# Edge stage of a graph attention kernel: gathers wait on VectorE's messages of the pair six back

## What is computed

```python
Q, K, V = (x @ W for W in (Wq, Wk, Wv))            # 6250 x 512, 8 heads of 64
score = einsum('ehd,ehd->eh', K[src], Q[dst]) / 8
score = exp(clip(score, -5, 5))[..., None]
msg = V[src] * score
wV, Z = segment_sum(msg, dst), segment_sum(score, dst)
h = x + wV / (Z + 1e-6)
y = (h - mean(h, 0)) * rsqrt(var(h, 0) + 1e-5) * gamma + beta
out = layernorm(x + y, axis=-1)
```

## Time and profile before

| | us |
|---|---|
| median of three runs | 1907.17 |
| profiled execution | 1908.01 |
| its span, first to last instruction | 1906.1 |
| edge stage, first gather to last sums | 452 to 1760 |

### The profile page before, as it was taken

How to read it: one execution, slowest core, us unless ns; L and a number is a source line. 1 busy time by engine, 2 the same in 40 slices (tenths; PEclk the granted TensorE clock), 3 DMA queues, 4 the chain that set the end, 5 groups by cost and what they waited for, 6 DMA issues and landing times.

```text
span 1906.1 us, 41424 instructions
## 1 busy us (share of the span) xinstructions
PE 1861.6 (98%) x7904; PEld 1362.2 (71%) x8014; DVE 1697.0 (89%) x2454; ACT 1367.5 (72%) x4602; POOL 1291.3 (68%) x1473
## 2 busy tenths in 40 slices
PE   7999999998999999999999999999999999999897
PEld 4555555554888888878888888888888888887333
DVE  6677755644999999999999999999999999999888
ACT  0002000002999999999999999999999999998857
POOL 0205666103777888788888888888888888885677
PEclk9999999999999999999999999999999999999999
DMA  5547788546999999999999999999999999999307
GB/s 183 162 151 250 288 319 274 186 161 231 357 358 356 362 367 358 346 351 368 368 356 353 352 366 369 354 355 355 366 361 358 360 355 365 370 358 370 122 33 287
DMA packets 184521, 589.09 MB, mean 309 GB/s; under 512 B 28480, under 2 KB 30240, under 8 KB 184480
## 3 DMA queue, kind: packets, MB, share of 16 engines
q0 software_dynamic: 135904, 465.14, 65.8%
q1 hardware_dynamic: 45120, 121.69, 17.8%
q10 hardware_dynamic: 3456, 1.78, 0.3%
HBM read 535.27 MB, written 78.91 MB: 322 GB/s over the span
## 4 chain that ended last, share of the span: by engine, by line
PE 74%; DVE 16%; issue 4%; DMA 4%; ACT 1%; POOL 1%; SPq 0%; DVEq 0%; ACTq 0%; POOLq 0%
PE acc L939 29%; PE places L342 22%; PE q_ps L923 17%; DVE kv L795 6%; DVE raw L806 5%; DMA kv<-kv_d,idx 2%; PE mm_ps L949 2%; PE banks L1151 1%; DVE stats L1288 1%; DVE agg L1281 1%; PE mm_ps L951 1%; PE places L402 1%; DMA q_tile<-xb_d 1%; POOL kv L751 1%; PE banks L1142 1%
## 5 line engine op out<-in xcount | busy, mean ns | idle before, releaser
L751 POOL DMA_INDIRECT kv<-kv_d,idx x880 | 887.0, 1008 | 339.2 <-issue 204.8
L846 ACT ACTIVATE kv<-kv 128x64 f32<-128x64 f32 x3520 | 889.0, 335 | 14.3
L939 PE MATMUL acc<-kv,mm_sb 128*128 128x260 f32 x3520 | 845.6, 383 | 4.1 <-POOL kv L714 2.2
L939 PEld LDWEIGHTS acc<-kv,mm_sb 128*128 128x128 f32 x3520 | 654.3, 190 | 137.9 <-issue 32.8
L923 PE MATMUL q_ps<-q_tile,mm_sb 128*128 x1760 | 559.2, 439 | 5.6 <-DVE kv L795 4.9
L795 DVE TENSOR_TENSOR kv<-q_ps,kv 128x1024 f32<-128x1024 f32 x440 | 536.1, 1218 | 14.0 <-PE q_ps L923 7.0
L806 DVE TENSOR_REDUCE raw<-kv 128x16 f32<-128x1024 f32 x440 | 532.2, 1210 | 0.0
L923 PEld LDWEIGHTS q_ps<-q_tile,mm_sb 128*128 128x128 f32 x1760 | 328.6, 189 | 74.4 <-DVE kv L795 20.8
L714 DVE TENSOR_TENSOR kv<-kv 128x384 f32<-128x384 f32 (+1 forms) x440 | 271.6, 617 | 0.1
L857 ACT ACTIVATE mm_sb<-mm_ps,less 128x1024 fp32r<-128x1024 f32 x220 | 241.2, 1096 | 13.1 <-remote 10.1
L435 ACT COPY p<-places 128x768 f32<-128x768 f32 x23 | 18.4, 798 | 243.5 <-PE places L342 243.5
(11 more groups left out here) (171 smaller groups left out, 1358.6 us busy)
## 6 DMA issues: line engine op xcount, KB each, us to landing
q_tile<-q_d SPq DMA_DIRECT2D x49, 512.0 KB, 7.2
kv<-kv_d,idx POOLq DMA_INDIRECT x880, 6.2
kv_d<-kv_a SPq DMA_DIRECT2D x25, 512.0 KB, 5.5
xb<-in_x POOLq DMA_DIRECT2D x49, 256.0 KB, 4.3
xb_d<-xb POOLq DMA_DIRECT2D x49, 256.0 KB, 3.7
out_rows<-agg SPq DMA_DIRECT2D x49, 256.0 KB, 2.1
x_sb<-in_xT SPq DMA_DIRECT2D x24, 512.0 KB, 7.9
q_d<-q_a SPq DMA_DIRECT2D x24, 512.0 KB, 4.1
```

The lines of the kernel that those rows point to most:

```text
L751: pool.indirect_dma_start(kv[:, s, u, 0:2 * DIM], None, kv_d, bass.IndirectOffsetOnAxis(idx[:, s, u:u + 1], 0), bounds_check=N_NODES - 1, ...
L846: return act.activation(v, v, ACT.Copy, scale=kv[:, s, u, 2 * DIM + h:2 * DIM + h + 1])
L939: last = pe.matmul(acc[:, bass.ds(par, 1), DIM - (1 - n) * HALF:DIM + n * HALF], m, kv[:, sc, u, DIM + n * HALF:DIM + (n + 1) * HALF], sta ...
```

## The change

`IDX_PAIRS` goes from 4 to 2, so an index copy takes four columns in place of eight and is made in every even step, for the couple of pairs that begins two pairs ahead. The wait of the gathers on `s_qx` goes; in its place, ahead of the wait on the index copy, stands one on a new semaphore `s_w`, which VectorE's messages raise, in place of their increment of `s_v`: the gathers of pair q wait until VectorE's messages of pair q-6 are made (`GATHER_LAG` = 6). VectorE makes these in its step q-4, behind the product of pair q-4, so the slot is free by then. TensorE waits for `s_v` with one less, and beside it for `s_w`. GpSimd's messages stand behind the second gather, as they did.

```diff
-IDX_PAIRS = 4
+IDX_PAIRS = 2
@@
-        s_t_first = sem("s_t_first")
+        s_t_first, s_w = sem("s_t_first"), sem("s_w")
@@
-        POOL_LAG = 5
+        POOL_LAG, GATHER_LAG = 5, 6
@@ gather
                     if s % IDX_PAIRS == 0:
                         wait_apart(pool, s_idx[s // IDX_PAIRS], fills)
-                    wait_apart(pool, s_qx, q + 5 - RING)
                 pool.indirect_dma_start(kv[:, s, u, 0:2 * DIM], None, kv_d,
@@ step of GpSimd
                 sp, fp = at(s, fills, -POOL_LAG)
+                if there(q):
+                    wait_apart(pool, s_w, q + 1 - GATHER_LAG)
                 if there(q):
                     gather(q, s, fills, 0)
@@ step of VectorE
                     dve.wait_ge(s_exp[s2], f2)
-                    weigh(dve, s2, ACT_HEADS, HEADS - ACT_HEADS - (POOL_HEADS if s % 2 == 0 else 0)).then_inc(s_v[s2], 1)
+                    weigh(dve, s2, ACT_HEADS, HEADS - ACT_HEADS - (POOL_HEADS if s % 2 == 0 else 0)).then_inc(s_w, 1)
@@ step of TensorE
-                    pe.wait_ge(s_v[sc], (2 if sc % 2 else 3) * fc)
+                    pe.wait_ge(s_v[sc], (1 if sc % 2 else 2) * fc)
+                    pe.wait_ge(s_w, c + 1)
                     pe.wait_ge(s_evict, tiles[1] + 1)
```

## The result

The changed kernel takes 2042.77 us (median; 2040.2 to 2045.17) against 1907.41 of the kernel before (now four runs): a ratio of 1.0707 [1.0689, 1.0726], so 135 us more. The sign was right, the size was far off: 36 us were forecast, and 2043 lies outside 1906 to 1960. The profiled execution took 2043.35, its span 2041.6.

The account below looks back on a forecast made before the run. TensorE was taken to hold the edge stage's pace, 11.62 us for four pairs (mean 11.69). A new loop of 12.03 us added 0.34 us over 107 turns, 36 us, giving a median of 1943 us, range 1906 to 1960.

Parts of the forecast that it names:

- the odd loop: Edge stage, odd pairs: new closed loop from VectorE's message through gathers, GpSimd's message and TensorE, 12.03 us for four pairs.
- (a): GpSimd, odd pairs: from the end of VectorE's message to the start of the gather it gates, 0.79 us.
- (b): GpSimd, odd pairs: from the first gather's start to the start of GpSimd's message, 2.29 us.
- (c): GpSimd's message in odd pairs: 0.41 us because it starts behind VectorE's, ending about 0.5 us after it.
- the rival that frees the engine: GpSimd's message no longer overlaps VectorE's and shrinks from 0.65 to 0.41 us; kernel gets faster, 1898 us, chance 0.10.
- The even loop is just under the odd one: Edge stage, even pairs: their own loop through the gate takes 11.92 us, under 12.03, so adds nothing.
- The present disturbances vanish in the slack: Edge stage: present disturbances such as tile changes are absorbed, so the cost is 36 us, not 44.
- listed as waiting for VectorE in most pairs: Expected profile sign: GpSimd's gathers wait on VectorE's L714 line in most pairs, starting about 0.8 us after its messages.
- The added wait: TensorE's extra semaphore wait per pair: 0.05 us when behind GpSimd's message, at most 0.1; nothing for odd pairs.
- The copies and the start of the stage at nothing: GpSimd's 110 more index copies gain or cost nothing further; the edge stage's start costs 0, give or take 2 us.
- data not late: Rival denied here: VectorE's products wait for gathers' landing, 4 us more, perhaps 22 further, up to 1965 us, chance 0.08.
- the gate costs nothing: Rival: gathers start 0.30 us after VectorE's message, so the loop is 11.54 us; time 1907 us, chance 0.12.

Follow-up runs that it names:

- one-input kernel: Changed kernel with VectorE's messages replaced by a reduction reading one SBUF operand, its heads of V left unweighted: 1974.24 us against 1908.91, ratio 1.0346.
- the old order with the same edit: Kernel before, old gate kept, with VectorE's messages replaced by a reduction reading one SBUF operand: 1900.58 us, ratio 0.9955.

## Why the prediction was right or wrong

**The mechanism was right.** The gate at VectorE's message closes a loop through GpSimd's message and TensorE's sums. TensorE's new idle time stands where it was forecast: over the whole kernel 98.6 us before the sums, released by GpSimd's message (35 were forecast). It is not 0.15 to 0.2 us before the sums of every even pair: over 600 to 1500 us there are 72 waits for 139 even pairs, of 0.9 us each, so one in a turn.

```profile
L941 PE MATMUL acc<-kv,mm_sb 128*128 128x260 f32 x3520 | 865.0, 389 | 99.7 <-POOL kv L714 98.6
```

With the old gate it falls to 4.2 us in the 900, with the message ahead of the gathers to none.

**The sum, term by term**, for the odd loop that the forecast adds up, in the one-input turn above (1204.55 to 1216.68) and the changed one (1229.39 to 1242.29):

| step | forecast | one input | changed |
|---|---|---|---|
| (a) message's end to gather | 0.79 | 0.83 | 1.19 |
| (b) gather to GpSimd's message | 2.29 | 2.32 | 2.66 |
| (c) the message | 0.41 | 0.41 | 0.41 |
| (d) to the sums, with the added wait | 0.45 | 0.39 | 0.39 |
| (e) sums to product | 3.39 | 3.50 | 3.48 |
| (f) product to the next message's end | 4.70 | 4.68 | 4.77 |
| sum | 12.03 | 12.13 | 12.90 |

Over 107 turns: 36 us forecast + (12.13 - 12.03) x 107 = 11 for the clean loop + (12.29 - 12.13) x 107 = 17 for disturbances + (12.95 - 12.29) x 107 = 71 for held gathers, 135 in all. The parting of the last two goes by what the one-input kernel gave back; the changed kernel's own mean lies only 0.05 us over its turn of 12.90.

*Step (b), gather to message, is the one that failed*, and the same mistake made (a) too short: every gather was priced at about 1 us. Step (b) measured 2.66 us, not 2.29; the even pair's step from its first gather to the odd pair's, 3.15 and not 2.73, so that the odd pair's first gather, queued behind it, started 1.19 us after its gate and not 0.79. I took 2.29 us from gathers of 0.99 and 1.03 as they ran in the earlier trace rows, where GpSimd's queue had shifted them away from VectorE's messages. The new gate starts the gathers 0.97 us after the end of a message, 1.39 us later comes the pair's second, and that is where VectorE's next message starts. In the turn above the two held gathers cost 0.38 us (1.76 against 1.38) and 0.34 us (1.36 against 1.02) of 12.90 - 12.13 = 0.77. I had read the stretched message of GpSimd (0.65) as the rival that frees the engine, and did not ask the same of the gathers. Long gathers stood in the trace of before as well; the order of time, before the stretch of the earlier trace rows:

```profile
1201.71 0.68 DVE L714 TENSOR_TENSOR kv<-kv 128x512 f32<-128x512 f32 x1
...
1202.05 1.21 POOL L751 DMA_INDIRECT kv<-kv_d,idx  x1 [0.30 <-issue]
```

*"The even loop is just under the odd one"* was wrong for the changed kernel, if nearly right without held gathers. With one input both take 12.13, and the odd pair's first gather starts 0.38 us behind the one ahead of it and not at the queued 0.30, so its own gate just holds it. With held gathers it starts at the queued 0.30: what sets the pace is the even gate, behind which both held gathers lie (the even pair's second and the odd pair's second). The copy that meets VectorE's message (0.49 us at 1234.85, not 0.20) lies outside these steps.

*"The present disturbances vanish in the slack"* was wrong. In the one-input kernel the mean lies 0.16 us above the clean turn (12.29 against 12.13), and before it lay 0.07 above (11.69 against 11.62). Most of it are the stops before every hundredth gather: with the loop closed GpSimd has no slack to take them in, while the old order with the same edit has idle times of up to 2.04 us there and not one such long turn.

*Step (a)*: 0.79 was forecast, 0.97 from the message's end to the gather in the even loop, where I had 0.89. In the odd loop it is 0.83 without held gathers. The gathers that wait show 0.72 to 0.90 us of idle time in the rows above, but they are one in eight (73 of 555 with more than 0.5 us), and 72 of these are listed under "issue"; the list names VectorE for 68 of 556 gathers, with 12.5 us. So my sign "listed as waiting for VectorE in most pairs" was wrong while the wait was there.

*The added wait*: I took 0.05 us in the loop, with 0.1 as the bound, and nothing in the odd pairs for their cover. The cover holds (1.92 us in both kernels). In an even pair the price is 0.09 to 0.11 us, at or just over the bound: sums to product take 3.50 in the turn of 12.13 and not 3.39. Without the gate it is paid in both even pairs of a turn, 0.15 us and 12 us of the median, a third of what I forecast for the whole change.

*The message*: 0.41 was forecast, and 0.41 stands in the turn above; it ends at 1233.65, 1.30 us after VectorE's, not 0.5. The pace was to be 3.0 us a pair and is 3.24; the DMAs below 355 GB/s, and they carry 325.

*The copies and the start of the stage at nothing, data not late*: right.

**The rivals.** That the gate costs nothing (0.12) holds on the chips whose pace is longer anyway, not here. The gain from a freed GpSimd (0.10) fell by the very effect that it was built on: the hold moved from the message (663 to 450 ns in the mean) to the gathers (1009 to 1095), and there are four of these to each message. On the chips of the result's pace late data show to any size in one run only, the one with the message first.

No whole kernel that was run beats the kernel before by more than 0.3%: copies for two pairs alone give 0.9982, the message between the gathers 0.9978.

## What to carry to other kernels

When a change moves an instruction in time, lay its new start beside what the neighbour engines run then, and price it with the rows where it met them, not with its rows of now. Look for the longest row of a repeated instruction, not the median: here 1.21 us (1.31 at the most) among gathers of 0.99 said what a new order would pay every time. And before an engine's queue is tied to another's progress, add up the ring that this closes: with the slack gone, each 0.1 us in it was paid 107 times, and so were the rare stops that the slack had hidden.

## What was not expected of the hardware

- An indirect gather on GpSimd that starts while VectorE runs a product with two inputs in SBUF lasts 1.37 us in the mean and up to 1.46 instead of 0.99 to 1.05, and a copy of 128x4 int32 0.49 instead of 0.20. With one input all gathers stay within 0.986 to 1.042.
- A gather for which GpSimd waited idle started 0.97 us after VectorE's message ended, with 0.72 us of it after the engine's last instruction; queued ones stand 0.16 to 0.30 apart. The Trainium skill, "DMA: Bandwidth & Descriptors", section "Anatomy of one DMA — SWDGE (gpsimd) path", puts the sequencer's dispatch at about 50 ns; that alone doesn't account for it.
- One more wait a pair on TensorE against a register's value, with TensorE at 299 of 300 us, cost 0.15 us in four pairs, all of it in the even ones, though the list of waits shows next to nothing for it (2.5 us).
- Before every hundredth indirect gather GpSimd stands idle, for 2.00 to 2.04 us in the one-input kernel and for 0.38 to 1.93 in the kernel before.
- The same program takes 1907 us on one chip and 2089 on another, and a gate that costs 7% on the one costs nothing on the other.
